# A two-layer graph network on one core: the second layer's one-hot of the low bits goes to POOL, and three of 21 evictions of counts per group go to DVE

## What is computed

```
h = relu(layernorm(x))
deg = segment_sum(ones, dst);  dinv = rsqrt(deg)
feat[d] = sum over the edges (s -> d) of (h @ W_gcn)[s] * dinv[s] * dinv[d]
x = x + relu(feat @ W1 + b1) @ W2 + b2
```

## Time and profile before

| | |
|---|---|
| median of three runs | 6518.5 us (6517.94 to 6523.41) |
| the profiled execution | 6520.64 us, its span 6518.9 us |
| PE busy | 5654.6 us (87%), 38038 instructions |
| DVE busy | 4173.9 us (64%), 13072 instructions |
| ACT busy | 3822.2 us (59%), 7170 instructions |
| POOL busy | 3237.0 us (50%), 3406 instructions |

### The profile page before, as it was taken

One profiled execution on the slowest core, in us unless ns is written; L12 is line 12 of the kernel. 1 busy time (PEld: TensorE's weight loads), 2 busy tenths in 40 slices (PEclk: granted clock), 3 DMA queues, 4 the chain that ended last, 5 costly groups with the idle time before them and its releaser, 6 DMA issues. The chain is left out here.

```text
span 6518.9 us, 128731 instructions
## 1 busy us (share of the span) xinstructions
PE 5654.6 (87%) x38038; PEld 4382.9 (67%) x38038; DVE 4173.9 (64%) x13072; ACT 3822.2 (59%) x7170; POOL 3237.0 (50%) x3406
## 2 busy tenths in 40 slices
PE   6755559999999999999999999977799999999998
PEld 5311127777777777777777777765477777777777
DVE  5577764545454544445454444553799999999996
ACT  3566644434444444444444444433699999999996
POOL 3577757777777777777777777753000000000000
PEclk8555555555555555555555555555799999999998
DMA  4444433333333333333333333321000000000001
GB/s 155 137 123 124 124 83 74 74 76 75 76 75 76 74 76 74 74 76 75 75 75 76 74 75 75 74 79 30 18 2 2 2 2 2 2 2 2 2 2 62
DMA packets 297570, 400.07 MB, mean 61 GB/s; under 512 B 146679, under 2 KB 203015, under 8 KB 296247
## 3 DMA queue, kind: packets, MB, share of 16 engines
q1 hardware_dynamic: 193543, 233.00, 12.1%
q0 software_dynamic: 103344, 158.83, 11.5%
HBM read 333.74 MB, written 57.67 MB: 60 GB/s over the span
## 5 line engine op out<-in xcount | busy, mean ns | idle before, releaser
L932 POOL DMA_INDIRECT gbuf<-a_tab,idxb x2688 | 2580.4, 960 | 859.0 <-issue 812.3
L1718 ACT ACTIVATE nf<-psum 128x600 bf16<-128x600 f32 x3234 | 1824.2, 819 | 4.8 <-PE psum L1709 4.8
L1017 PEld LDWEIGHTS psum<-rhs,lhs 128*128 128x128 f32 x6448 | 1434.3, 327 | 365.8 <-issue 365.8
L1017 PE MATMUL psum<-rhs,lhs 128*128 128x96 f32 x6448 | 1628.7, 434 | 13.5 <-DVE rhs L975 13.5
L1038 ACT ACTIVATE msg<-pre 128x384 f32<-128x384 f32 x806 | 421.8, 523 | 1991.2 <-DVE pre L1030 1988.7
L1030 DVE TENSOR_TENSOR pre<-psum,gbuf 128x384 f32<-128x384 f32 x806 | 448.2, 556 | 1613.6 <-issue 1130.0
L1709 PE MATMUL psum<-x_all 128*128 128x300 bf16 x6468 | 1358.8, 291 | 121.6 <-DVE x_all L1702 44.6
L1061 PE MATMUL psum<-oh,msg 128*97 128x32 f32 x6448 | 1171.1, 344 | 282.4 <-ACT msg L1038 276.7
L1061 PEld LDWEIGHTS psum<-oh,msg 128*97 128x97 f32 x6448 | 1134.0, 282 | 364.1 <-ACT msg L1038 358.7
L1701 DVE TENSOR_SCALAR x_all<-x_all,dstrel 128x600 bf16<-128x600 f16 x3234 | 1193.8, 369 | 87.4 <-PE psum L1709 63.0
L1731 PE MATMUL psum<-x_all,nf 128*128 128x96 bf16 x15400 | 1074.4, 205 | 1.0 <-ACT nf L1718 1.0
(11 more groups left out here) (198 smaller groups left out, 3340.3 us busy)
## 6 DMA issues: line engine op xcount, KB each, us to landing
gbuf<-a_tab,idxb POOLq DMA_INDIRECT x3224
x_all<-dst_row SPq DMA_DIRECT2D x403, 128.0 KB
x_all<-attr_parts SPq DMA_DIRECT2D x807, 36.0 KB
x_all<-attr_parts SPq DMA_DIRECT2D x1209, 24.0 KB
spilled<-gbuf SPq DMA_DIRECT2D x134, 192.0 KB, 1.9
gbuf<-spilled SPq DMA_DIRECT2D x134, 192.0 KB
x_all<-b_tab SPq DMA_DIRECT2D x806, 12.0 KB
attr_parts<-sT SPq DMA_DIRECT2D x72, 136.0 KB, 1.9
```

The lines of the kernel that those rows point to most:

```text
L932: g.indirect_dma_start(gbuf[:, k % 4, t, :], None, a_tab[:, :], bass.IndirectOffsetOnAxis(ap=idxb[:, k % 4, t:t + 1], axis=0)).then_inc(g_ ...
L1017: ins = pe.matmul(ps_m(k)[:, t, :], lhs[:, k % 2, t * TILE:(t + 1) * TILE], rhs[:, k % 2, :], start=True, stop=True)
L1718: act.activation(adj[:, g % 2, :, j * SLOT:(j + 1) * SLOT].rearrange("p (b h) s -> p b h s", b=2), ps_a(n).rearrange("p b (h s) -> p b h s ...
```

## The change

POOL now builds `o_lo`, for all 3234 tiles, in the same order and under the same wait for `a_mm`. It signals with a semaphore of its own (`l_oh`), and PE waits for it as well as for `e_oh`. DVE builds `o_key` alone and, of each seven tiles, evicts the fourth (n mod 7 = 3): j = 3, 10 and 17 of every group. It does so two tiles later in its order, at j = 5, 12 and 19, after the one-hot of that tile. ACT leaves these out and keeps 18 of 21. The wait for `b_mm` stands before ACT's first two evictions of a group and before each of DVE's.

```
-        def edge_onehots(dve, n):
+        def on_dve(n):
+            return n % 7 == 3
+
+        def kept_by_dve(n):
+            return (n + 3) // 7
+
+        def key_onehot(dve, n):
             if n >= 3:
                 dve.wait_ge(a_mm, n - 2)
-            dve.tensor_scalar(o_key[:, n % 3, :], iota_k, key_f[:, n:n + 1], None, ALU.is_equal)
-            dve.tensor_scalar(o_lo[:, n % 3, :], iota_l, lo_f[:, n:n + 1], None, ALU.is_equal).then_inc(e_oh, 1)
+            dve.tensor_scalar(o_key[:, n % 3, :], iota_k, key_f[:, n:n + 1], None, ALU.is_equal).then_inc(e_oh, 1)
+
+        def low_onehot(g, n):
+            if n >= 3:
+                g.wait_ge(a_mm, n - 2)
+            g.tensor_scalar(o_lo[:, n % 3, :], iota_l, lo_f[:, n:n + 1], None, ALU.is_equal).then_inc(l_oh, 1)
 
         def tile_counts(pe, n):
+            pe.wait_ge(l_oh, n + 1)
             pe.wait_ge(e_oh, n + 1)
-            if n >= 3:
-                pe.wait_ge(a_ok, n - 2)
+            if n >= 3 and on_dve(n - 3):
+                pe.wait_ge(v_ok, kept_by_dve(n - 2))
+            elif n >= 3:
+                pe.wait_ge(a_ok, n - 2 - kept_by_dve(n - 2))
...
         def keep_counts(act, n):
+            if on_dve(n):
+                return
             act.wait_ge(a_mm, n + 1)
-            if j == 0 and g >= 2:
-                act.wait_ge(b_mm, g - 1)
+            if n >= 2 * GT and n % GT in (0, 1):
+                act.wait_ge(b_mm, n // GT - 1)
...
+        def keep_counts_too(dve, n):
+            if not on_dve(n):
+                return
+            dve.wait_ge(a_mm, n + 1)
+            if n >= 2 * GT:
+                dve.wait_ge(b_mm, n // GT - 1)
+            kept, counts = counts_to_keep(n)
+            dve.tensor_copy(kept, counts).then_inc(v_ok, 1)
...
                     for g in range(NG + 2):
                         for j in range(GT):
                             if g < NG:
-                                edge_onehots(dve, g * GT + j)
+                                key_onehot(dve, g * GT + j)
+                            if 0 <= g * GT + j - 2 < TD:
+                                keep_counts_too(dve, g * GT + j - 2)
                             if g >= 2 and j == 2:
                                 group_parts(dve, g - 2)
                             if g >= 2 and j == 12:
```

More of the change, by code:

```diff
@@ L1670, in gnn_kernel @@
         k_first = sem("k_first")
+        l_iota = sem("l_iota")
         k_v = sem("k_v")
@@ L1678, in gnn_kernel @@
         a_ok = sem("a_ok")
+        v_ok = sem("v_ok")
+        l_oh = sem("l_oh")
         b_mm = sem("b_mm")
@@ L1711, in tile_counts, with counts_to_keep @@
             ins.then_inc(a_mm, 1)
+        def counts_to_keep(n):
+            g, j = n // GT, n % GT
+            return (adj[:, g % 2, :, j * SLOT:(j + 1) * SLOT].rearrange("p (b h) s -> p b h s", b=2),
+                    ps_a(n).rearrange("p b (h s) -> p b h s", s=SLOT))
         def keep_counts(act, n):
-            g, j = n // GT, n % GT
+            if on_dve(n):
+                return
             act.wait_ge(a_mm, n + 1)
-            if j == 0 and g >= 2:
-                act.wait_ge(b_mm, g - 1)
-            act.activation(adj[:, g % 2, :, j * SLOT:(j + 1) * SLOT].rearrange("p (b h) s -> p b h s", b=2),
-                           ps_a(n).rearrange("p b (h s) -> p b h s", s=SLOT), ACT.Copy).then_inc(a_ok, 1)
+            if n >= 2 * GT and n % GT in (0, 1):
+                act.wait_ge(b_mm, n // GT - 1)
+            kept, counts = counts_to_keep(n)
+            act.activation(kept, counts, ACT.Copy).then_inc(a_ok, 1)
+        def keep_counts_too(dve, n):
[4 more added lines that the diff above has]
+                dve.wait_ge(b_mm, n // GT - 1)
+            kept, counts = counts_to_keep(n)
+            dve.tensor_copy(kept, counts).then_inc(v_ok, 1)
         def group_sums(pe, g, q):
@@ L1726, in group_sums @@
                     pe.wait_ge(t_rest, 2)
-                pe.wait_ge(a_ok, GT * (g + 1))
+                pe.wait_ge(v_ok, kept_by_dve(GT * (g + 1)))
+                pe.wait_ge(a_ok, GT * (g + 1) - kept_by_dve(GT * (g + 1)))
                 if g >= 1:
@@ L1770, in _ @@
                         g.memset(adj[:, b, :, QS:P], 0.0).then_inc(a_zero, 1)
+                    g.wait_ge(l_iota, 1)
+                    for n in range(TD):
+                        low_onehot(g, n)
                 @block.tensor
@@ L1816, in _ @@
                     link(dve.tensor_copy(iota_k, iota_f))
-                    link(dve.tensor_copy(iota_l, iota_p[:, :]))
+                    dve.tensor_copy(iota_l, iota_p[:, :]).then_inc(l_iota, 1)
                     dve.wait_ge(t_part, 1)
```

## The result

The changed kernel took 6961.35 us as the median of four runs (6954.51 to 6962.97), against 6520.95 us (6517.94 to 6523.73) before: a ratio of 1.0671, 95% interval 1.0658 to 1.0684. That is 440 us more, where I had forecast 45 more and put the end of the range at 6690.

The account below looks back on a forecast made before the run. ACT was taken as the bound at 11.85 us per group. The tile intervals summed to 11.59, plus 0.24 and 0.31 for port collisions made 12.14, 154 x 0.29 = 45 us more: 6563 us for the median, range 6472 to 6690.

Parts of the forecast that it names:

- What bounds the kernel before: In the changed stage: ACT sets the pace with 21 evictions of 0.564 us, 11.85 us per group.
- The eviction on DVE: Each of DVE's three evictions per group: 0.78 us for 600 columns, 0.70 until DVE's next start.
- The queue behind the evictions: In DVE's in-order queue, one-hots wait behind evictions: 0.42 us lost at tile 13, 0.10 at tile 20.
- I take 0.34: POOL's one-hot of 128 columns: 0.34 us, taken from a select, between 0.237 and 0.40.
- a rival with 0.13: Port becomes the bound, above 6690 us: over 12 of 21 collide fully, or POOL passes 0.51 us per tile; chance 0.13.
- One collision costs DVE up to 0.24 us: At the shared SBUF ports: POOL's instruction holds up DVE's `o_key` by up to 0.24 us (0.14 to 0.30).
- rows 9 and 10: Node-stage trace rows: a DVE TENSOR_SCALAR took 0.723 us beside POOL, median 0.169; the reduce ahead kept its 0.55.
- the ledger without ports: Sum of a group's tile intervals, queue steps included, without a cost of the ports: 11.59 us.
- I had charged 0.55: Port collisions per group: 0.24 us at tile 13 and 0.31 at the head, raising 11.59 to 12.14 us.
- POOL has gone on to tiles 14 and 15: Before tile 13's `o_key`, POOL runs ahead, and its one-hot of tile 15 meets that `o_key`: + 0.24 us.
- The estimate of 0.39 us: POOL's one-hot by the skill's not unrolled comparison loop, 0.22 us plus about 0.17 fixed; sum about 6595 us.
- Its lower figure of 0.28: POOL's one-hot by the skill's unrolled comparison loop, 0.11 us plus about 0.17 fixed; sum given as about 6510 us.

Follow-up runs that it names:

- e4: The changed kernel with POOL comparing only the first 32 of 128 columns: stage 1799.2 us, ratio to before 0.9957.
- e6: e4 with DVE's evictions moved from tiles 3, 10 and 17 of a group to 5, 12 and 19: stage 1773.1 us, 11.52 per group.
- e5: The kernel before, with 72 POOL instructions in six forms added at the start of the last stage: the change's form took 0.577 us from start to start.
- e12: The changed kernel with DVE's one-hot in one-port form and no evictions on DVE: stage 1882.3 us, 12.23 per group.
- e1: The changed kernel with no evictions on DVE, ACT evicting all 21 tiles of a group: stage 2206.8 us, ratio to before 1.0497.
- e3: The changed kernel with DVE's compared row in three runs of 200 with gaps, the one-port form: stage 1921.1 us, 12.48 per group.
- e8: The changed kernel with POOL building every third tile's low one-hot, DVE the others and evicting tiles 7 and 16: stage 1832.5 us, ratio to before 1.0016.
- e11: The kernel before, with 2400 POOL one-hots of 128 columns beside it that nobody reads or waits for: stage 1824.2 us.
- e7: The kernel before with POOL idle and one eviction of 21 (tile 16) on DVE: stage 1774.1 us, ratio 0.9933.
- e10: e7 with `o_slot` built on POOL and two evictions per group on DVE (tiles 7 and 16): stage 1802.4 us, ratio to before 0.9968.
- e2: The changed kernel with `o_lo` back on DVE and POOL idle, DVE still evicting three of 21 tiles: stage 1931.8 us, ratio to before 1.0135.
- e9: e7 with `o_slot`, one comparison per group, built on POOL: stage 1773.4 us, ratio to before 0.9936.

## Why the prediction was wrong

- **What bounds the kernel before** was right: ACT, with PE behind it at 0.51 us per tile.
- **The eviction on DVE** at 0.78 us: measured 0.782.
- **The queue behind the evictions**, 0.42 us at tile 13 and 0.10 at tile 20: right. e4 shows 0.93 and 0.64, and e6 takes the first away by moving the evictions. The 0.81 us from the eviction's start to the add and the 0.21 to the next one-hot stand in the changed kernel as well (5509.84, 5510.65, 5510.86). But there POOL covers the step: its one-hot of tile 13 is ready 0.7 us after DVE's, and the queue comes back in another form, as the 1.43 us of POOL beside three one-hots in a row.
- **"I take 0.34", between 0.237 and 0.40, is the term that failed first.** POOL's one-hot takes 0.60 us alone, 0.577 from start to start (e5; 0.582 in e12). It lies half above my upper end, which was built from another operation's rate. At that pace POOL passes ACT's 0.564 before any port is shared: 60 us of the 440 (e12). I had named the point ("when POOL alone passes 0.51 us per tile") and kept it in a rival with 0.13.
- **"One collision costs DVE up to 0.24 us" is the step that failed.** The ports are held exclusively as rows 9 and 10 showed, but they showed one case, a POOL instruction of 0.99 us that was already under way. With short one-hots on both sides DVE's grew by 0.02 us and POOL's by 0.12 on average, from 0.577 to 0.70 start to start, and by 0.83 (1.43 in place of 0.60) where DVE issues three in a row. Since POOL was the bound, that went into the time in full: 324 us (e1 less e12), taken away again by DVE's one-port form (e3). It would have failed with a short POOL instruction too: in e4 DVE's grew by 0.01 us and the group took 0.10 more than the ledger without ports, where I had charged 0.55. What decides who is held when both ask, no run separates. By the recorded starts it isn't who began first, since POOL had begun first both where it was held itself (792 times in the changed kernel) and where it held DVE (271 times in e8); that POOL paid most is shown by e1, e8 and e11.
- **Tile 13: "POOL has gone on to tiles 14 and 15"** was wrong as well for the changed kernel. POOL had no lead there: it was building the one-hot of tile 13 itself while DVE's queue caught up, and PE waited for that.
- So the sign was right by luck, for two wrong reasons: I charged the ports to an engine with room, and took the engine without room for one that is hidden.

The rule of the Trainium skill on the shared ports (SBUF — State Buffer, Who interferes with whom) says that a DVE instruction in a 2-port mode contends with POOL and that one with a single SBUF input outside these modes doesn't, and that the loser waits for the whole instruction. The runs agree: the two-port comparison meets POOL, the eviction out of PSUM does not (0.60 us beside the CAST), nor does the one-port form (e3, 0.600), and POOL's ends stand at a fixed distance behind DVE's. The same section says that the one who issues first gets the pair. The recorded starts don't bear that out, as above; whether an engine takes the ports later than its recorded start, no run here shows. The estimate of 0.39 us that the prediction worked out from the Trainium skill (GPSIMD Engine Reference, Performance pitfalls for Q7 kernels) was too low by a third; the measurement decides. (Its lower figure of 0.28 gives 11.90 us per group by the prediction's own sum, and so about 6526, not 6510.)

## What to carry to other kernels

Before an instruction goes to an engine on which the trace doesn't have it, measure it there by itself: a guess from the engine's nearest other operation was wrong by 75%, and it alone decided which engine is the bound. Work given to POOL beside DVE's two-port comparisons must have room for POOL's instruction at its stretched length (0.70 to 0.86 us here for 0.60 alone), not at its own. And an eviction in an in-order queue costs what stands behind it: one per group gained 49 us, two gained 20 and three lost 109 (e7, e10, e2; e10 has `o_slot` on POOL as well, which by e9 changes nothing).

## What was not expected of the hardware

POOL's TENSOR_SCALAR on 128 columns takes 0.60 us in bf16 and fp32, comparison and addition alike (e5); a column of the bf16 comparison costs 2.5 ns, and a number per partition 0.08 us. In nine kernels the first or the second of these instructions took 3.5 to 3.9 us, once (3.76 in the changed one); in e5 and e11 none did, and the cause is open. Where one of the two instructions was held at the ports, it ended at a fixed distance behind the other: POOL's 0.14 to 0.15 us after DVE's (792 of 796 in the changed kernel), DVE's 0.17 us after POOL's (271 of 273 in e8). A DVE comparison of 600 fp16 numbers costs 0.38 us in its two-port form and 0.52 in its one-port form, and the slower form made this kernel 341 us faster.
